# A new order of work in the slots of a fused Mamba and mixture-of-experts kernel

## The reference, cut to what matters

```
x = x + mamba(layernorm(x))          # mamba(x) itself returns x + out
x = x + moe(layernorm(x))

mamba: xn = layernorm(x);  u, z = split(xn @ W_in)          # 512 channels each
       u = silu(causal conv of 4 taps over u)
       dt, B, C = split(u @ W_xp);  dt = softplus(dt @ W_dt + b_dt)
       h = exp(dt * A) * h + (dt * u) * B;  y = sum over 16 states of h * C, + u * D
       out = (y * silu(z)) @ W_out
moe:   top 2 of 8 experts per token; sort the tokens by expert;
       silu(x @ gate_e) * (x @ up_e) @ down_e, weighted, added back to its token
```

## Time and profile before

| what | value |
|---|---|
| median of 3 runs | 2396.81 us (2390.99 to 2398.17) |
| the profiled execution: time, span | 2390.97 us, 2389.1 us |
| busy share of the span | PE 76%, PEld 39%, DVE 83%, ACT 72%, POOL 82% |
| largest groups, busy us | `drive` L1301 985.3; `decay` L945 673.1; the scans L1089 454.7 + 477.8 + 163.3 + 155.3 |
| chain that ended last | PE 35%, POOL 20%, issue 17%, ACT 16%, DVE 7%, DMA 4% |
| DMA | 369.34 MB, mean 155 GB/s |
| mean granted TensorE clock | 0.869 |

### The profile page before, as it was taken

How to read it: one execution, slowest core, us unless ns; L and a number is a source line. 1 busy time by engine, 2 the same in 40 slices (tenths; PEclk the granted TensorE clock), 3 DMA queues, 4 the chain that set the end, 5 groups by cost and what they waited for, 6 DMA issues and landing times.

```text
span 2389.1 us, 32277 instructions
## 1 busy us (share of the span) xinstructions
PE 1805.6 (76%) x7630; PEld 934.7 (39%) x7630; DVE 1987.7 (83%) x2756; ACT 1719.3 (72%) x3273; POOL 1957.3 (82%) x1284
## 2 busy tenths in 40 slices
PE   6557777686868788787968888786878878665885
PEld 2113222243434444443534444443534444243542
DVE  0499989999898989899898989999898989999311
ACT  5778677877887777877887677877878678754232
POOL 2688787979989897998989898998979898997333
PEclk9789788798989888897989889898989889777998
DMA  2545354575767676685758576686757667597332
GB/s 73 132 103 128 87 140 102 151 185 144 199 152 188 154 188 147 175 198 146 188 147 196 151 190 167 163 202 154 194 137 188 161 176 175 156 249 225 77 59 35
DMA packets 217979, 369.34 MB, mean 155 GB/s; under 512 B 31040, under 2 KB 86592, under 8 KB 217664
## 3 DMA queue, kind: packets, MB, share of 16 engines
q1 hardware_dynamic: 192208, 333.56, 54.0%
q0 software_dynamic: 25584, 33.71, 7.2%
HBM read 285.05 MB, written 83.01 MB: 154 GB/s over the span
## 4 chain that ended last, share of the span: by engine, by line
PE 35%; POOL 20%; issue 17%; ACT 16%; DVE 7%; DMA 4%; POOLq 0%; ACTq 0%; DVEq 0%
POOL arena L1301 7%; PE yps L692 5%; PE ring L594 4%; PE ring L602 4%; DMA out<-yt,xt 4%; PE p_g L724 4%; ACT dA L945 4%; DVE dA L1089 4%; PE ring L622 3%; POOL sorted_x L1339 3%; POOL arena L1309 2%; PE ring L610 2%; POOL out L1349 2%; POOL rst L1273 2%; PE p_a L704 2%
## 5 line engine op out<-in xcount | busy, mean ns | idle before, releaser
L1301 POOL TENSOR_TENSOR arena<-arena,b_bc 128x2048 f32<-128x2048 f32 x256 | 985.3, 3849 | 67.6 <-PE yps L692 63.7
L945 ACT ACTIVATE dA<-arena,a_s 128x512 f32<-128x512 f32 x1024 | 673.1, 683 | 135.7 <-DVE arena L1098 106.2
L1089 DVE TENSOR_TENSOR_SCAN dA<-dA,arena 128x512 f32<-128x512 f32 x384 | 454.7, 1215 | 137.7 <-ACT dA L945 103.1
L1089 DVE TENSOR_TENSOR_SCAN dA<-dA,carry,arena 128x512 f32<-128x512 f32 x384 | 477.8, 1275 | 39.2 <-POOL arena L1301 23.3
L692 PE MATMUL yps<-arena,const_s 128*32 128x512 f32 x2048 | 325.6, 712 | 210.8 <-POOL arena L1309 135.0
L1098 DVE TENSOR_TENSOR arena<-dA,c_bc 128x1024 f32<-128x1024 f32 x256 | 313.6, 1225 | 8.8
L1349 POOL DMA_INDIRECT out<-yt,xt x135 | 215.5, 1597 | 115.6 <-DMA out<-yt,xt 62.0
L1309 POOL TENSOR_TENSOR arena<-arena,c_bc 128x511 f32<-128x511 f32 (+1 forms) x256 | 296.0, 1156 | 15.7 <-DVE arena L1089 14.8
L594 PE MATMUL ring<-arena 128*128 128x512 f32 x488 | 258.6, 656 | 58.5 <-ACT arena L853 34.3
L724 PEld LDWEIGHTS p_g<-xT,w_e 128*128 128x128 f32 x1680 | 230.7, 215 | 28.9 <-issue 26.1
L724 PE MATMUL p_g<-xT,w_e 128*128 128x128 f32 x1680 | 236.1, 300 | 6.5 <-DVE hT L1222 6.5
(11 more groups left out here) (165 smaller groups left out, 2967.6 us busy)
## 6 DMA issues: line engine op xcount, KB each, us to landing
arena<-dt_d SPq DMA_DIRECT2D x512, 256.0 KB
w_e<-in_w_moe SPq DMA_DIRECT2D x105, 512.0 KB
dt_d<-arena SPq DMA_DIRECT2D x128, 256.0 KB, 2.3
w_e<-in_w_moe SPq DMA_DIRECT2D x105, 256.0 KB
xt<-sorted_x SPq DMA_DIRECT2D x135, 129.0 KB
b_bc<-bc_d SPq DMA_DIRECT2D x256, 64.0 KB, 2.1
c_bc<-bc_d SPq DMA_DIRECT2D x256, 64.0 KB
xs<-in_x SPq DMA_DIRECT2D x16, 512.0 KB, 6.9
```

The source lines that it names most:

```text
L945: act.activation(dA[:, j, :], rep_dt[:, c % 2, j, :], ACT.Exp, scale=a_s[:, n, j:j + 1]).then_inc(s_exp, 1)
L1089: return dve.tensor_tensor_scan(out_ap, dA[:, j, :], hs[:, u % 3, j, :], init, ALU.mult, ALU.add)
L1301: pool.tensor_tensor(hs[:, u % 3], rep_dtu[:, c % 2], b_bc[:, g, :].unsqueeze(1).to_broadcast([P, J, T]), ALU.mult).then_inc(s_dbu, 1)
```

## The change

The same operations with the same operands stand in another order and in other slots. `TAIL_AT` and one tile of batch 14 move; the scatters go out two per slot in all batches; `MAKES` and `TAKES` are new; the written order within a slot is new on all five engines; the first `decay` is now j = 0, and scan 0 waits for one exponential where it waited for two. The tables of batch 0 follow the new ones in their late entries and are cut here.

```diff
@@ -42,7 +42,7 @@
 LATE_FROM = UN * NQ + 1
 TILE_AT = [17, 20, 22, 24, 26, 28, 29, 31]
-TAIL_AT = 19
+TAIL_AT = 15
 class Batch:
@@ -54,14 +54,14 @@
         self.nk = LAST if q == NQ - 1 else 2 * QT if q > 0 else 1
         self.tiles = before.tiles + before.nk if before else 0
         rows = [(k, t) for k in range(2) for t in range(QT)]
-        a_slot = 2 if q >= NQ - 2 else 1
+        a_slot = 2 if q >= NQ - 2 else 2
         self.scatter = {row: self.ready + SCATTER + n // a_slot for n, row in enumerate(rows)}
         self.swap = self.scatter[0, QT - 1]
         if q == NQ - 1:
             first = max(self.ready + TAIL_AT, before.at[-1] + 1)
             self.at = [first + k for k in range(self.nk)]
         elif q == NQ - 2:
-            self.at = [self.ready + k for k in [18, 20, 21, 22, 23, 25, 26, 28]]
+            self.at = [self.ready + k for k in [18, 20, 21, 22, 23, 25, 26, 29]]
         else:
             self.at = [self.ready + k for k in TILE_AT[2 * QT - self.nk:]]
@@ -93,32 +93,31 @@
-MAKES = {(-19, 0): ["X0", "X1"], (-19, 4): ["U0"], (-18, 0): ["U1"], (-18, 3): ["W0"], (-17, 4): ["W1"], (-15, 3):
-         ["U2"], (-14, 2): ["U3"], (-14, 4): ["W2"], (-12, 3): ["W3"], (-11, 4): ["P0"], (-10, 4): ["D0"], (-9,
-         0): ["Z0"], (-8, 0): ["Z1"], (-7, 0): ["Z2"], (-7, 1): ["Z3"], (-7, 2): ["D1"], (-2, 1): ["D2"], (1,
-         0): ["D3"], (16, 4): ["O0"], (17, 4): ["O1"], (19, 4): ["F0"], (20, 3): ["F1"], (21, 1): ["R0"], (23,
-         2): ["K0"]}
-
-
-TAKES = {(-20, 3): ["X0"], (-19, 0): ["X1"], (-19, 4): ["U0"], (-18, 0): ["U1"], (-17, 0): ["W0"], (-16, 0): ["W1"],
-         (-15, 3): ["U2"], (-14, 3): ["U3"], (-13, 4): ["W2"], (-11, 1): ["W3", "SU"], (-10, 1): ["P0"], (-10,
-         4): ["D0", "E0"], (-9, 2): ["Z0"], (-8, 0): ["Z1", "L0"], (-8, 4): ["Z2"], (-7, 2): ["Z3"], (-7, 4):
-         ["D1"], (-6, 2): ["SZ"], (-5, 2): ["E1"], (-3, 2): ["L1"], (-2, 3): ["D2"], (-1, 0): ["E2"], (0, 3):
-         ["L2"], (1, 2): ["D3"], (1, 3): ["E3"], (2, 2): ["L3"], (17, 0): ["O0"], (18, 2): ["O1"], (20, 1):
-         ["F0"], (20, 2): ["F1"], (21, 3): ["R0"], (23, 3): ["K0"]}
+MAKES = {(-20, 1): ["X0", "X1"], (-20, 4): ["U0"], (-18, 0): ["U1"], (-18, 4): ["W0"], (-17, 4): ["W1"], (-14, 1):
+         ["U2"], (-14, 4): ["U3"], (-13, 3): ["W2"], (-12, 4): ["W3"], (-10, 0): ["P0"], (-10, 2): ["D0"], (-9,
+         2): ["Z0"], (-9, 3): ["Z1"], (-8, 3): ["Z2", "Z3"], (-7, 4): ["D1"], (-2, 2): ["D2"], (1, 0): ["D3"],
+         (16, 3): ["O0"], (17, 1): ["O1"], (20, 2): ["F0"], (20, 3): ["F1"], (21, 2): ["R0"], (23, 3): ["K0"]}
+
+
+TAKES = {(-20, 4): ["X0"], (-19, 0): ["X1"], (-19, 1): ["U0"], (-18, 0): ["U1"], (-17, 1): ["W0"], (-16, 1): ["W1"],
+         (-14, 4): ["U2"], (-13, 0): ["U3"], (-13, 4): ["W2"], (-11, 2): ["W3", "SU"], (-10, 2): ["P0"], (-10,
+         4): ["D0"], (-9, 0): ["E0"], (-9, 2): ["Z0"], (-8, 0): ["Z1", "L0"], (-8, 2): ["Z2"], (-7, 2): ["Z3"],
+         (-7, 3): ["D1"], (-6, 1): ["SZ"], (-5, 3): ["E1"], (-3, 2): ["L1"], (-2, 2): ["D2"], (-2, 4): ["E2"],
+         (0, 0): ["L2"], (1, 2): ["D3", "E3"], (2, 2): ["L3"], (17, 2): ["O0"], (18, 2): ["O1"], (20, 1):
+         ["F0"], (20, 2): ["F1"], (21, 4): ["R0"], (24, 0): ["K0"]}
...
@@ -536,29 +535,27 @@
             for s in range(FIRST, TOTAL_SLOTS):
                 q, n = s // UN, s % UN
                 front = 0 <= q + 1 < NQ
-                for g, k in tiles_in(s + 1):
-                    load_tile(g, k)
-                if q >= 0 and front and n == 9 or s == -13:
-                    store_bc(q + 1)
-                for g, k in tiles_in(s - 1, False):
-                    load_down(g, k)
-                if n == 4 and 0 <= q - 1 < NQ:
+                if n == 5 and 0 <= q - 1 < NQ:
                     store_x2(q - 1)
-                if n == 6 and 2 <= q + 2 < NQ:
+                if n == 5 and 2 <= q + 2 < NQ:
                     load_x(q + 2)
-                if q == NQ - 1 and n in (4, 5, 6, 7, 9, 10, 13, 14):
-                    load_late((4, 5, 6, 7, 9, 10, 13, 14).index(n))
-                if n == 0 and 0 <= q < NQ:
-                    load_c(q, G - 1)
-                if front and n >= 13:
-                    load_c(q + 1, n - 13)
                 if q >= 0 and front and n >= 12:
                     load_b(q + 1, n - 12)
                 if s == -12:
                     for g in range(G):
                         load_b(0, g)
-                for p, k in pieces(s, (-6, -1, 2, 5), (-10, -1, 3, 5)):
+                if q >= 0 and front and n == 6 or s == -13:
+                    store_bc(q + 1)
+                for g, k in tiles_in(s - 1, False):
+                    load_down(g, k)
+                for g, k in tiles_in(s + 1):
+                    load_tile(g, k)
+                if q == NQ - 1 and n in (4, 5, 6, 7, 9, 10, 13, 14):
+                    load_late((4, 5, 6, 7, 9, 10, 13, 14).index(n))
+                for p, k in pieces(s, (-5, 0, 3, 7), (-10, -1, 3, 7)):
                     store_dt(p, k)
+                for g, k in tiles_in(s + 1, False):
+                    load_expert(g, k)
                 if 0 <= q < NQ and n in (0, 4, 8):
                     load_rep(q, n // G + 1, (0, 1))
                 if q >= 0 and front and n == 12 or s == -9:
@@ -567,12 +564,14 @@
                     load_rep(q, (n - 1) // G + 1, (2, 3))
                 if q >= 0 and front and n - 1 == 12 or s == -9:
                     load_rep(q + 1, 0, (2, 3))
-                for g, k in tiles_in(s + 1, False):
-                    load_expert(g, k)
                 if q == NQ - 1:
                     for e, at in enumerate((11, 11, 12, 12, 13, 13, 14, 14, 15)):
                         if n == at:
                             no_tokens(e)
+                if n == 0 and 0 <= q < NQ:
+                    load_c(q, G - 1)
+                if front and n >= 13:
+                    load_c(q + 1, n - 13)
             sp.wait_ge(s_add, 16 * TILES)
             sp.wait_ge(s_x2w, 16 * NQ)
@@ -773,14 +772,14 @@
             for s in range(FIRST, TOTAL_SLOTS):
                 for item in made_in(s, 0):
                     make(item)
-                if 0 < s <= UN * NQ:
-                    weigh(s - 1)
                 for g, k in tiles_in(s - 3, False):
                     down(g, k)
                 for g, k in tiles_in(s - 4, True):
                     late_down(g, k)
                 for g, k in tiles_in(s - 3, True):
                     late_turn(g, k)
+                if 0 < s <= UN * NQ:
+                    weigh(s - 1)
                 for g, k in tiles_in(s, False):
                     tile_transpose(g, k)
                 for g, k in tiles_in(s, True):
@@ -1000,50 +999,50 @@
             diagonals(0)
             for s in range(FIRST, TOTAL_SLOTS):
                 q, n = s // UN, s % UN
-                if 0 <= s < UN * NQ and q % 2 == 0:
-                    keep01(s)
-                if 0 <= s + 1 < UN * NQ:
-                    decay(s + 1, 1)
-                for p in range(NQ):
-                    if s == UN * (p + 1) + 7:
-                        gap_exp(p)
-                if 0 <= s + 1 < UN * NQ:
-                    decay(s + 1, 0)
                 for p in range(NQ):
                     if s == ALL[p].swap + 1:
                         second_weight(p)
                 for item in taken_in(s, 0):
                     take(item)
+                if 0 <= s < UN * NQ and q % 2 == 0:
+                    keep01(s)
+                if 0 <= s + 1 < UN * NQ:
+                    decay(s + 1, 0)
                 for p in ahead(s, 12, -9):
                     norm_x(p)
+                if 0 <= s + 1 < UN * NQ:
+                    decay(s + 1, 1)
                 if 0 <= s + 1 < UN * NQ:
                     decay(s + 1, 3)
                 for item in taken_in(s, 1):
                     take(item)
+                for g, k in tiles_in(s - 3, True):
+                    late_take(g, k)
+                for p in range(NQ):
+                    if s == UN * (p + 1) + 7:
+                        gap_exp(p)
                 for item in taken_in(s, 2):
                     take(item)
+                if n == 3 and 0 <= q - 1 < NQ:
+                    norm_x2(q - 1)
                 if 0 <= s < UN * NQ and q % 2 == 0:
                     keep2(s)
-                if n == 3 and 0 <= q - 1 < NQ:
-                    norm_x2(q - 1)
-                for g, k in tiles_in(s - 3, False):
+                if 0 <= s < UN * NQ and q % 2 == 0:
+                    keep3(s)
+                for g, k in tiles_in(s - 4, True):
                     take_y(g, k)
                 for item in taken_in(s, 3):
                     take(item)
+                for item in taken_in(s, 4):
+                    take(item)
                 if 0 <= s + 1 < UN * NQ:
                     decay(s + 1, 2)
-                for g, k in tiles_in(s - 4, True):
-                    take_y(g, k)
-                for item in taken_in(s, 4):
```

(41 more changed lines are left out.)

## The result

The kernel after ran 2387.78 us in the median of 5 runs (2382.05 to 2388.39), the kernel before 2397.61 (2390.99 to 2400.09) beside it: ratio 0.9954, 95% interval 0.9935 to 0.9972. That is 11 us less, beyond the 0.3% that can be told; forecast were 48. The profiled execution ran 2387.78 us with a span of 2385.9 (before 2389.1), at a mean granted clock of 0.865 (0.869).

The account below looks back on a forecast made before the run. VectorE and GpSimd were taken as two nearly full engines, each limited by its own work and hand-overs. -35 - 28 + 15 = -48 us from 2391 gave 2343, with 5.8 on top 2349 us; range 2315 to 2402.

Parts of the forecast that it names:

- part 4: TensorE's order, down ahead of weigh: later weighing hidden until drive needs it; zero, bounds -10 and +60.
- Rival C: TensorE: down waits for ACT's xT eviction, so weighing ends 2.2 us later, two slots a batch; 2411 us, chance 0.12.
- Part 1: POOL, slots 8 to 0: 83.0 us of work and waits fall to 80.0; 35 us gained, bounds 0 to 56.
- Part 2: Second output product made earlier in slot 1: bn_stats' wait falls from 2.7 to 0.7; 28 us gained, bounds 0 and 38.
- Part 3: ACT's order: scan 0 waits for one exponential, other work delays later ones; +15 us, from -17 to +35.
- Parts 5 and 6: SP's order of loads and stores, and the tail: each zero, bounds -5 and +10, and -8 and +5.
- Part 7: DVE: first norm's moments move from end of slot 10 to start of slot 9; 2.2 us moved, zero in sum.
- Rival D: Shared port: gap<-mx or hot on DVE waits until a drive ends, each batch; 52 us lost, 2401, chance 0.05.
- rival E: Each wait turns into another, mostly exponentials behind norm_x, Silu and keep3; 2397 us, no measurable change, chance 0.09.

Follow-up runs that it names:

- e11: Kernel after with TensorE's order of before, weigh of the last slot ahead of a tile's down product: 2366.83 us, 0.9866 of the kernel before.
- e3: Kernel before with POOL's new order, two scatters per slot, SP's new order and the moved tile of batch 14: 1.0083 of the kernel before.
- e15: e11 with POOL's order, the scatters' slots and SP's order of before: 0.9996 of the kernel before.
- e7: Kernel before with the second output product moved (U2, U3, W2 later, O0 taken in place 2): 1.0013 of the kernel before.
- e16: e11 with the second output product and U2, U3, W2 made in the places of before: 1.0079 of the kernel before.
- e4: Kernel before with the new MAKES and TAKES, ACT's new order and scan 0 waiting for one exponential: 1.0031 of the kernel before.
- e18: e11 with ACT's order of before and scan 0 waiting for two exponentials again: 1.0131 of the kernel before.
- e13: Kernel before with only TensorE's new order, down ahead of weigh: 1.0059 of the kernel before.
- e12: Kernel after with DVE's order of before, moments(0) at the end of slot 10, activate at the end of a slot: 0.9943 of the kernel before.
- e10: Kernel after without plus_relu's addition, 5.4 us of POOL's work per batch: 0.9902 of the kernel before.
- e2: Kernel after with POOL's weigh(s) ahead of deviation(0) in slot 11: 1.0054 of the kernel before.
- e8: Kernel after with the last four scatters of batches 0 to 13 spread over slots 12 and 13: 0.9941 of the kernel before.
- e17: Kernel before with the edits of e3 and e7 together: 1.0025 of the kernel before.
- e1: Kernel after with the logarithm (L0) ahead of Z1 on ACT in slot 8: 0.9966 of the kernel before.

## Why the prediction was wrong, step by step

| part | forecast, us | alone on the kernel before | within e11 |
|---|---|---|---|
| 1 with 5, POOL's and SP's order | -35 | +20 (e3) | -31 (e15) |
| 2, second output product | -28 | +3 (e7) | -51 (e16) |
| 3, ACT's order | +15 | +7, with 2 (e4) | -64 (e18, old order under the new tables) |
| 4, TensorE's order | 0 | +14 (e13) | +21 (e11) |
| 7, moments on DVE | 0 | not tried | +3 (e12, within the kernel after) |
| sum or whole | -48 | | -32 without part 4, -11 with it |

**The step that failed is part 4.** It put TensorE's order at zero because a weighing 1.1 us later is hidden by the two slots until `drive` needs it. The delay was not the 1.13 us of `down` but the wait in front of it. Rival C named that mechanism, `down` behind the xT eviction, and I gave it 0.12 with 4.4 us per batch; measured are 1.7 per batch. It priced ACT's work ahead of xT by an ordinary slot, m2 + 0.7 + 0.4. In slot 11 it is a Silu between two table loads, 4.5 us more, and such a wait holds the weighing once or twice per batch. Its sign came as written: `drive` waits for TensorE more often than once a batch, 24 times in 13 batches. The runs change the order as a whole, so that the wait and not `down`'s own length is what costs is read from the rows and not from a run of its own. With 21 us in place of the zero the sum is -27, and -11 was measured.

**Part 1: the size held, the reason did not.** Within the rest it is worth 31 us of the 35. But the count of slots 8 to 0 as one pot of 83.0 us that shrinks to 80.0 is refuted: the stretch lasts 83.4 us in e11, 79.4 in e15 without part 1, and e15 is the slower kernel. e10 says the same: GpSimd's sum of work isn't the bound by itself. By DVE's slots, e11 gains 2.5 us over e15 in slots 0 to 7 and loses 0.5 in the others, 3.2 of it lost to `gated` in slot 12, a wait that the forecast has no term for; the wait for exponentials is 4.0 us per batch in e15 and 1.3 in e11. Removing `gated`'s wait paid in neither e2 nor e8. How work moved on POOL brings the exponentials in time no run shows; e3 and e17 show only that it doesn't pay while the logarithm is late.

**Part 2:** the wait went, from 2.7 to 0.1 us per batch where 0.7 was forecast. Its worth was 51 us within the rest and 3 alone.

**Part 3** was not priced by itself in any run. Put into the kernel before with the ring's tables it loses 7 us (e4), the sign that was forecast; taken out under the new tables it costs 64 (e18), and there TensorE and `round_off` wait on ACT too, where the bound of -17 took the scans' waits alone. **Parts 5 and 6** were not isolated. **Part 7** was zero within the measurement.

**Rival D** (shared port) came true in some batches, and its sign (over 1.5 us) was met: `hot` rose in the mean from 0.79 us to 1.55 while `gap<-mx` fell from 0.81 to 0.52, half a microsecond more per batch. Behind that mean are two cases. In 4 of the 13 steady batches `hot` starts behind a `drive` and lasts 3.24 us, in the others at most 0.84 (kernel after, DVE, then POOL):

```profile
1199.41 3.24 DVE L1134 TENSOR_TENSOR hot<-ix,const_s 128x64 f32<-128x64 uint32 x1
```

```profile
1198.76 3.81 POOL L1300 TENSOR_TENSOR arena<-arena,b_bc 128x2048 f32<-128x2048 f32 x1
```

`hot` ends 0.08 us behind the `drive`, in all four cases. In e11 it is 7 of 13 batches, and slot 7 is the one that e11 lengthens. The forecast's rival had this in every batch; its 0.6 us of waiting before holds for `gap<-mx` and not for `hot`, which takes 0.51 us at least and 0.79 in the mean, so 0.3. A version that keeps `hot` clear of the `drive` was not tried. In slot 7 of the batch shown before, `hot` (1064.81, 0.83 us) ends within 0.1 us of POOL's L1312 (1064.46, 1.09 us). By the Trainium skill (SBUF — State Buffer, section Who interferes with whom) a VectorE instruction with two SBUF inputs contends with a GpSimd instruction that reads SBUF, and whichever comes second is blocked until the other ends; this case agrees, 3.24 us behind a `drive` and 0.83 behind the shorter L1312.

**What the sum left out.** Batches 0 and 1 take 9.4 us more, with or without part 4 (252.0 in e11). Both orders add to it: e3 takes 4.7 more there and e4 8.0. One of its places: before, the exponential stood on ACT ahead of E's three operations (L877 to L882) and DVE went on at 91.83 with no wait; after, it stands behind them (kernel after, DVE in slot 0 of batch 0):

```profile
93.30 1.23 DVE L1088 TENSOR_TENSOR_SCAN dA<-dA,arena 128x512 f32<-128x512 f32 x1 [2.15 <-ACT dA L944]
```

The rest of the 9.4 us was not traced. I had counted 14 batches and said nothing of the first two. In the e11 trace batches 2 to 15 are 38.1 us shorter, 2.7 per batch where 48 / 14 = 3.4 were summed. That this is near the forecast is in part luck, since the parts are worth other sums than it gave them.

**The adding of terms** is the fault under all of these. Put into the kernel before one at a time, the parts make +20, +3 and +7 us (the last holds part 2 too); taken out of the whole one by one they are worth 31, 51 and 64, which is 146 where the whole has 32. In e1, e2, e7, e8 and e10 a wait or work that was taken away came back as other waits, as rival E has it. The reading that fits all of them is that POOL, ACT, TensorE and DVE come to a unit within a few microseconds of each other, so that removing one wait pays only if the other arrivals move too, and undoing one part costs much of what the others gave; no run measures those distances. The forecast was right that the whole pays, and by how much without part 4 only roughly (32 of 48); its terms, each priced as if the others stood still, are no measure of the parts.

## What to carry to other kernels

When an instruction is moved ahead of another in an engine's order, price the wait in front of it, in the slot where its producer is latest (here behind a Silu with two table loads), not its own length. Where several engines arrive within a few microseconds, a part tried alone tells little: test it by taking it out of the whole, and then one order at a time. A count of one engine's work between two points is a bound only if taking work out shortens the time; that is a test of one run. And a mean over batches can hide two cases: look at the single instructions, as with `hot`.

## What the runs showed of the hardware that was not expected

The z product in slot 8 (four accumulating 128x512 products) was counted as 1.9 us and took 3.54; before, four such took 1.88 us at 1080.14 and 3.09 at 1075.85. Kernel after, the stretch of that product and the one ahead of it (columns as above):

```profile
1070.90:1074.50 3.60, 3.59 (x8) 1.09 (x12) 3.35 (x23) 0.01 (x1) 2.99 (x3) 0.54 1.06 314
1058.00:1069.00 11.00, 8.67 (x52) 4.79 (x52) 10.13 (x22) 8.12 (x16) 9.40 (x4) 1.00 0.71 195
```

The granted clock was 0.54 of full there, near the lower of its two levels (1.2 of 2.4 GHz), after 1.00 in a stretch in which TensorE was busy 8.67 of 11.00 us. So the logarithm behind it came 1.6 us later than counted. And on GpSimd, busy 90% of the stretch, 5.4 us less work per batch brought 12 us in all and 1.0 us more per batch cost 8 to 10, each with an uncertainty of 6 or more: it is, as far as these runs tell, neither free nor the bound.

A VectorE operation of 128x64 (`hot`) that took 0.51 or 0.52 us in seven steady batches of the kernel before took 3.24 us in four of the kernel after, where it started 0.65 us behind the start of a GpSimd operation of 3.81 us.
